# One rank product for two tiles: prefix sums made once at the head of a sort on a Trainium2 core

## The reference

```
ex1 = e * x[src];  ex2 = e * x[dst]
mi = zeros.at[dst].add(ex1);  mo = zeros.at[src].add(ex2)
h = concat([mi, mo, x]); h = tanh(h @ W1 + b1); ... four times
x = layernorm(x + h)
R = relu(edge_weight @ w1 + b1) @ w2 + b2          # per edge
msg = tensor product of R, spherical harmonics of edge_attr_3, x[src]
x = layernorm(x + zeros.at[dst].add(msg))
```

## Time and profile before

| what | value |
|---|---|
| median of 3 runs | 2183.33 us (2181.03 to 2185.21) |
| the profiled execution, its own time | 2181.47 us |
| its span, first to last instruction | 2179.7 us |
| busy in the span | PE 1313.5 (60%), DVE 1099.9 (50%), ACT 628.1 (29%), POOL 1255.6 us (58%) |
| mean granted TensorE clock | 0.741 |
| gathers L457 | 392, from 3.9 to 1205.8 us, 1.0 us each |
| scatters L462 | 392, from 65.9 to 1234.2 us, 1.0 us each |
| rank products L756, L757 | 392 each, from 63.4 to 632.2 us, granted clock 0.50 to 0.60 in 50 us stretches |

### The profile page before, as it was taken

The page is one execution under the profiler, slowest core; times in us unless marked ns, Lnnn a source line. Parts: engine busy times, 40 slices in busy tenths (PEclk is TensorE's granted clock), DMA queues, the critical chain, the costliest instruction groups (busy, mean ns, idle before and its releaser), DMA issues.

```text
span 2179.7 us, 23910 instructions
## 1 busy us (share of the span) xinstructions
PE 1313.5 (60%) x6086; PEld 938.6 (43%) x6086; DVE 1099.9 (50%) x3121; ACT 628.1 (29%) x1642; POOL 1255.6 (58%) x1315
## 2 busy tenths in 40 slices
PE   5644554232315566333332267999959999999564
PEld 4421332111113444233322155666636777777553
DVE  9543562232322222344332164777745777777576
ACT  0000000000001111000000296666634444443595
POOL 6466676666664566666666510333348888883144
PEclk8555555555557778566555598999978999999666
DMA  1011011111115555344431354455432333333486
GB/s 32 21 29 29 27 29 30 31 28 31 28 32 151 148 152 161 108 114 125 125 108 54 88 151 118 141 154 158 145 95 51 94 92 95 92 94 83 123 218 166
DMA packets 330295, 204.59 MB, mean 94 GB/s; under 512 B 32299, under 2 KB 318704, under 8 KB 330160
## 3 DMA queue, kind: packets, MB, share of 16 engines
q1 hardware_dynamic: 269008, 140.38, 24.2%
q0 software_dynamic: 35280, 49.84, 8.0%
q10 hardware_dynamic: 25872, 12.85, 2.0%
HBM read 124.03 MB, written 78.92 MB: 93 GB/s over the span
## 4 chain that ended last, share of the span: by engine, by line
issue 43%; PE 36%; DVE 8%; another core or an unknown queue 5%; POOL 4%; DVEq 2%; DMA 1%; SPq 1%; ACT 0%; POOLq 0%; ACTq 0%
PE bank L878 10%; PE bank L848 6%; PE bank L871 6%; DVE res L1083 5%; PE bank L801 3%; PE bank L803 2%; PE bank L841 2%; PE bank L839 2%; POOL out L529 2%; PE bank L887 2%; PE bank L855 2%; DVE woh L1062 2%; PE bank L811 1%; DVEq L1077 1%
## 5 line engine op out<-in xcount | busy, mean ns | idle before, releaser
L462 POOL DMA_INDIRECT placed<-pay,pos_i x392 | 395.6, 1009 | 317.2 <-issue 299.5
L457 POOL DMA_INDIRECT gat<-in_x,key_i x392 | 394.2, 1006 | 127.0 <-issue 116.4
L756 PE MATMUL bank<-oh,lower 128*128 128x196 bf16 x392 | 125.4, 338 | 301.4 <-issue 173.1
L811 PE MATMUL bank<-woh,pw 128*128 128x128 f32 x784 | 149.9, 362 | 260.5 <-DVE woh L1062 181.1
L1083 DVE TENSOR_TENSOR res<-res,bank 128x128 f32 x588 | 168.6, 287 | 258.2 <-remote 73.2
L982 DVE SCALAR_TENSOR_TENSOR junk<-iota,w_f,bank 128x196 f32<-128x196 f32 x392 | 147.7, 414 | 291.3 <-remote 158.5
L504 POOL DMA_INDIRECT gat<-x_d,src_i x196 | 256.8, 1310 | 59.5 <-issue 52.1
L811 PEld LDWEIGHTS bank<-woh,pw 128*128 128x128 f32 x784 | 136.0, 266 | 274.4 <-issue 221.6
L878 PE MATMUL bank<-prod,ident 128*128 128x280 f32 x896 | 217.8, 402 | 0.0
L756 PEld LDWEIGHTS bank<-oh,lower 128*128 128x128 bf16 x392 | 44.1, 113 | 381.1 <-issue 258.3
L878 PEld LDWEIGHTS bank<-prod,ident 128*128 128x128 f32 x896 | 171.7, 192 | 46.5 <-issue 0.6
(11 more groups left out here) (146 smaller groups left out, 2412.8 us busy)
## 6 DMA issues: line engine op xcount, KB each, us to landing
pw<-placed SPq DMA_DIRECT2D x588, 68.0 KB, 2.1
pw<-placed SPq DMA_DIRECT2D x98, 272.0 KB
xin<-in_x_t SPq DMA_DIRECT2D x98, 256.0 KB
hot_d<-woh SPq DMA_DIRECT2D x49, 256.0 KB
x_d<-res POOLq DMA_DIRECT2D x49, 256.0 KB, 3.8
oh<-hot_d SPq DMA_DIRECT2D x28, 448.0 KB
placed<-pay SPq DMA_DIRECT2D x28, 448.0 KB
out<-out ACTq DMA_DIRECT2D x49, 256.0 KB, 2.7
```

What stands on the lines that cost most here:

```text
L457: pool.indirect_dma_start(gat[:, t, :], None, x, bass.IndirectOffsetOnAxis(ap=key_i[:, 1 - c, t:t + 1], axis=0)).then_inc(s_gat[n // CHUNK ...
L462: pool.indirect_dma_start(placed[c].rearrange("t p r -> (t p) r"), bass.IndirectOffsetOnAxis(ap=pos_i[:, c, t:t + 1], axis=0), pay[i % 4][ ...
L756: pe.matmul(column(k), lower[:, :], oh[:, t, :], start=True, stop=False)
L811: ins = pe.matmul(quarter(bank, k), pw[i % 6][:, k, 0:P], woh[i % 3][:, k, :], start=True, stop=True)
```

## The change

Rank products are made for two tiles at a time: the moving operand is `oh[:, t:t + 2, :]`, 392 columns, into one PSUM bank; four such pairs are in flight, so the wait is for `place` of tile n-7. `s_rank` is counted up once for a pair. The second product is different too. A tile's sums over all tiles ahead are no longer made from `cnt_sb` and `pre` at each product. They are made once, in `sort_head`, as full sums for each row r of 49 and each of four heaps of tiles (heaps 2j and 2j+1 hold the even and odd tiles of pairs 49j to 49j+48), and copied by VectorE to `cum` as a bf16 value in partitions 0 to 63 and a bf16 remainder in partitions 64 to 112. The product then picks row r of both with a one-column matrix `pick`. `place` is as before but for the column it reads and the count that it waits for.

```
-HI, LO = 64, 96
+LO = 64
-        cnt_sb = sb_e("cnt_sb", [LO + 1, G, NW], BF16)
-        pre = sb_e("pre", [LO + 1, QT], BF16)
+        cnt_sb = sb_e("cnt_sb", [QT, 4, NW], BF16)
+        cum = sb_e("cum", [LO + QT, 2, 2 * NW], BF16)
+        pick = sb_e("pick", [LO + QT, QT], BF16)
+        under = sb_e("under", [QT, LO + QT], BF16)
+        upto = sb_e("upto", [QT, LO + QT], BF16)
...
+        def pair_of(n):
+            return psum[n // 2 % 4][:, 0:2 * NW]
+        def column(n):
+            return pair_of(n)[:, NW * (n % 2):NW * (n % 2) + NW]
+        def heap(t):
+            pair = t // 2
+            return 2 * (pair // QT) + t % 2, pair % QT
...
 count (PE)
-                    h, r = t // QT, t % QT
+                    m, r = heap(t)
...
 sort_head (PE)
-                for h in range(4):
+                for n in range(4):
                     for m in range(2):
-                        ins = pe.matmul(start_of(h), tot_sb[:, m, :], ubig[:, m, :], start=m == 0, stop=m == 1 and h == 0)
-                    for a in range(h):
-                        ins = pe.matmul(start_of(h), every[0:QT, :], cnt_sb[0:QT, a, :], start=False, stop=a == h - 1)
+                        pe.matmul(start_of(n), tot_sb[:, m, 0:LO + QT], ubig[:, m, :], start=m == 0, stop=False)
+                    for a in range(n - n % 2):
+                        pe.matmul(start_of(n), every[0:QT, 0:LO + QT], cnt_sb[:, a, :], start=False, stop=False)
+                    a = n - n % 2
+                    pe.matmul(start_of(n), (upto if n % 2 else under)[:, :], cnt_sb[:, a, :], start=False, stop=False)
+                    ins = pe.matmul(start_of(n), under[:, :], cnt_sb[:, a + 1, :], start=False, stop=True)
...
 rank (PE)
-                for k in range(G):
-                    t = G * (g % NG) + k
-                    wait(pe, s_pos, G * (g - 1) + k + 1)
-                    pe.matmul(column(k), lower[:, :], oh[:, t, :], start=True, stop=False)
-                    pe.matmul(column(k), pre[:, t % QT:t % QT + 1].broadcast_to([LO + 1, P]), cnt_sb[:, t // QT, :],
+                for k in range(0, G, 2):
+                    n, t = G * g + k, G * (g % NG) + k
+                    m, r = heap(t)
+                    wait(pe, s_pos, n - 6)
+                    pe.matmul(pair_of(n), lower[:, :], oh[:, t:t + 2, :].rearrange("p t w -> p (t w)"), start=True, stop=False)
+                    pe.matmul(pair_of(n), pick[:, r:r + 1].broadcast_to([LO + QT, P]), cum[:, m // 2, :],
                               start=False, stop=True).then_inc(s_rank, 1)
...
 constants (DVE)
-            fill.up(dve.tensor_scalar(pre[:, :], iota[0:LO + 1, 0:QT], pcol[0:LO + 1, :], None, ALU.is_gt))
+            (two comparisons for pick, two for under, two for upto)
-            fill.up(dve.memset(cnt_sb[:, :, :], 0.0))
-            done(fill)
-            for r in (HI, LO):
-                fill.up(dve.memset(pre[r:r + 1, :], 1.0))
...
 sort_starts (DVE)
-                for i in range(2):
-                    both = psum[i][:, 0:2 * NW].rearrange("p (h w) -> p h w", h=2)
-                    chain.up(dve.tensor_copy(cnt_sb[HI:LO + 1, 2 * i:2 * i + 2, :], both[HI:LO + 1]))
+                for h in range(2):
+                    chain.up(dve.tensor_copy(cum[:, h, :], psum[h][0:LO + QT, 0:2 * NW]))
                 done(chain)
-                    ins = dve.tensor_tensor(cnt_sb[LO:LO + 1, ...], both[LO:LO + 1], cnt_sb[LO:LO + 1, ...], ALU.subtract)
+                    ins = dve.tensor_tensor(cum[LO:LO + QT, h, :], psum[h][LO:LO + QT, 0:2 * NW], cum[LO:LO + QT, h, :], ALU.subtract)
...
 place (DVE)
-                    dve.wait_ge(s_rank, n + 1)
+                    dve.wait_ge(s_rank, n // 2 + 1)
-                    ... in1=column(k)
+                    ... in1=column(n)
```

More of the change, by code:

```diff
@@ L294, in quarter, with start_of @@
             return psum[bank][:, P * k:P * k + P]
[L296 to L301, removed]
+        def pair_of(n):
[5 more added lines that the diff above has]
+            return 2 * (pair // QT) + t % 2, pair % QT
+        def start_of(m):
+            return psum[m // 2][0:LO + QT, NW * (m % 2):NW * (m % 2) + NW]
         def first_rows(sp, to, c, b, landed):
@@ L544, in sort_head @@
                 act.wait_ge(s_cnt, c + 1)
-                for h in range(4):
-                    ins = act_copy(act, cnt_sb[0:QT, h, :], psum[h][0:QT, 0:NW])
+                for m in range(4):
+                    ins = act_copy(act, cnt_sb[:, m, :], psum[m][0:QT, 0:NW])
                 ins.then_inc(s_cnt_sb, 1)
@@ L717, in count @@
                 for t in range(U * n, U * n + U):
-                    h, r = t // QT, t % QT
-                    ins = pe.matmul(psum[h][0:QT, 0:NW], esel[:, QT - 1 - r:2 * QT - 1 - r], oh[:, t, :], start=r == 0, stop=r == QT - 1)
+                    m, r = heap(t)
+                    ins = pe.matmul(psum[m][0:QT, 0:NW], esel[:, QT - 1 - r:2 * QT - 1 - r], oh[:, t, :], start=r == 0, stop=r == QT - 1)
                 if n == NU - 1:
@@ L929, in _ @@
             fill.up(dve.tensor_scalar(lower[:, :], iota[:, 0:P], pcol[:, :], None, ALU.is_gt))
-            fill.up(dve.tensor_scalar(pre[:, :], iota[0:LO + 1, 0:QT], pcol[0:LO + 1, :], None, ALU.is_gt))
+            fill.up(dve.tensor_scalar(pick[0:LO, :], iota[0:LO, 0:QT], pcol[0:LO, :], None, ALU.is_equal))
+            fill.up(dve.tensor_scalar(pick[LO:LO + QT, :], iota[LO:LO + QT, 0:QT], pcol[LO:LO + QT, :], -float(LO), ALU.subtract, ALU.is_equal))
+            for a, op in ((under, ALU.is_gt), (upto, ALU.is_ge)):
+                fill.up(dve.tensor_scalar(a[:, 0:LO], iota[0:QT, 0:LO], pcol[0:QT, :], None, op))
+                fill.up(dve.tensor_scalar(a[:, LO:LO + QT], iota[0:QT, 0:QT], pcol[0:QT, :], None, op))
             fill.up(dve.memset(every[:, :], 1.0))
@@ L955, in sort_starts @@
                 dve.wait_ge(s_start, c + 1)
-                for i in range(2):
-                    both = psum[i][:, 0:2 * NW].rearrange("p (h w) -> p h w", h=2)
-                    chain.up(dve.tensor_copy(cnt_sb[HI:LO + 1, 2 * i:2 * i + 2, :], both[HI:LO + 1]))
+                for h in range(2):
+                    chain.up(dve.tensor_copy(cum[:, h, :], psum[h][0:LO + QT, 0:2 * NW]))
                 done(chain)
-                for i in range(2):
-                    both = psum[i][:, 0:2 * NW].rearrange("p (h w) -> p h w", h=2)
-                    ins = dve.tensor_tensor(cnt_sb[LO:LO + 1, 2 * i:2 * i + 2, :], both[LO:LO + 1], cnt_sb[LO:LO + 1, 2 * i:2 * i + 2, :], ALU.subtract)
+                for h in range(2):
+                    ins = dve.tensor_tensor(cum[LO:LO + QT, h, :], psum[h][LO:LO + QT, 0:2 * NW], cum[LO:LO + QT, h, :], ALU.subtract)
                 ins.then_inc(s_low, 1)
@@ L979, in place @@
                     c, t, n = g // NG, G * (g % NG) + k, G * g + k
-                    dve.wait_ge(s_rank, n + 1)
+                    dve.wait_ge(s_rank, n // 2 + 1)
                     wait(dve, s_pos, n - 3)
-                    dve.scalar_tensor_tensor(out=junk[n % 4][:, :], in0=iota[:, :], scalar=w_f[:, c, t:t + 1], in1=column(k),
+                    dve.scalar_tensor_tensor(out=junk[n % 4][:, :], in0=iota[:, :], scalar=w_f[:, c, t:t + 1], in1=column(n),
                                              op0=ALU.is_equal, op1=ALU.mult, accum_out=pos_f[:, c, t:t + 1]).then_inc(s_pos, 1)
```

## The result

| | kernel before | kernel after |
|---|---|---|
| time, median | 2183.59 us (2181.03 to 2185.21, 4 runs) | 2168.69 us (2165.59 to 2170.19, 4 runs) |
| ratio | | 0.9928, 95% interval [0.9914, 0.9941] |
| span of the profiled execution | 2179.7 us | 2163.6 us |

A forecast was written before the change was run, and what follows sets the result against it. GpSimd was taken to pace the rank stage, running dry while VectorE waits for late increments. Saving 25 us less the head's 1.6 gives -23.4 from 2181.47, so 2158.1, as a median 2160 us; range 2110 to 2187.

The forecast's parts named there:

- The bound: Rank stage: GpSimd sets the pace and runs dry at regular intervals; its holes, together 77 us, are on the path.
- What changes is the number of increments in a step: Rank stage: increments leave at the recorded times; a step needs 8, not 14, in chunk 0 and 6, not 10, in chunk 1.
- The prediction's own test: Rank stage: an unchanged number of GpSimd's holes would mean that increments were not the cost.
- if each hole grew: Rank stage: sign that the prediction is wrong; holes were to stay 4 to 5 us long.
- Chunk 0: First rank steps: a hole every third step, not every second, 5 instead of 7 over 15 steps; saves 9 us.
- Chunk 1: Later rank steps: a hole every fourth step, 6 instead of 8 over 24 steps, saves 10 us, first hole 2 more.
- The value taken: Rank stage saving: 25 us, between 21 and about 38 us, the latter if increments left every 2.0 us at any age.
- The growing intervals: Rank stage: increments leave ever later after GpSimd resumes, some 4.5 us each in the end; saving 21 us.
- The head: Before the first scatter: more bf16 sums, split fp32 sums and constants cost +1.6 us, all on the path.
- All holes close: Rival, rank stage: VectorE never falls behind, GpSimd runs at 10.26 us a step; median 2113 us, chance 0.18.
- slower: Rival, rank stage: delay goes with columns, a pair held twice as long as a tile, about 4 us; 2190 us, chance 0.10.
- Nothing comes of it: Rival, rank stage: holes needed at the same intervals whatever the increments; only the head's cost remains, 2185 us, chance 0.14.

The follow-up runs named there:

- the direct test: Kernel after with each pair's two 392-column products split into four of 196, one increment a pair, eight tiles ahead: 2021.24, 2020.96 and 2022.03 us, no delay in any.
- group 1: Four undelayed runs: kernel before with half the increments 1.0008; kernel after with extra increments 1.0020, one increment per four tiles 1.0021, four tiles ahead 1.0024.
- idle increments: Kernel after, each pair's first product also incrementing a semaphore nobody waits for: 2021.49 us without the delay, 2173.15 us with it.

## Why the prediction was right, and which of its steps was not

*The bound.* Right. GpSimd paces the stage, runs dry at regular intervals, and the time of its holes is on the path; the walks behind it moved by the same 16 us, and where the delay was absent the holes and the gain were absent with it.

*The mechanism by which the change helps.* Wrong. The failed step is "What changes is the number of increments in a step", that increments leave at the times of the rows whatever the products. With half the increments alone the time was 2186.61 us, where that step asks for 2163.5, and with the old number of them in the kernel after 2173.15, where it asks for 2183.5. The traces showed in its place that the slow part has the same pace in tiles in every variant (5 to 7 in 12 us), and that the first 8 us behind a restart hold 20 to 22 tiles, not 14, wherever the products are wide. Of the two other parts of the change, the lead accounts by the traces for 5.6 us at step 48 and not for the periods. The joined products, with the single wait of TensorE that comes with them, are what is left. That is argued and not shown: an inference by elimination from single runs on different chips, with one contrary number (2173.0), and the direct test never met the delay. Which part of the change saves the time stays open; that the number of increments alone does not is shown as far as one run each way can.

*Why it came out nearly right all the same.* By luck. The number of tiles between two holes was what mattered, and the assumed law gave nearly the right one: in chunk 0 a hole every third step, as forecast, 5 besides the first. The prediction's own test ("I am wrong if the number of holes is unchanged (then increments were not the cost)") could not tell the laws apart: joined products, lead and increments were all changed at once. Another of its signs did come true: it was to be wrong "if each hole grew", and each did, from 4.6 to 5.2 us in chunk 0 and from 5.2 to 7.0 in chunk 1. It had taken the delay to be gone 2.5 us after GpSimd's last DMA whatever came before; that is the value of chunk 0 before, and in the kernel after it was 3.6 us behind three steps and 5.5 behind five.

*Chunk 0.* Forecast -9; the holes besides the first went from 7 of 4.6 us in the mean to 5 of 5.2, which with two more ordinary gaps is -5.7; the first one, forecast to stay since it had its own cause, shrank from 4.61 to 1.20 (without the delay it was 1.79 in the kernel before and 2.05 in the kernel after); 2.2 us came back at step 24, where GpSimd now waits for chunk 1's payload (2.51 us); and 0.3 lies elsewhere. Sum -6.6.

*Chunk 1.* Forecast -12 with a hole of 4.9 us every fourth step; measured one of 7.0 every fifth, and -10.7. Of this, 3.0 us are the first hole (7.73 before, 0.77 and 4.28 after), where 2 were forecast. In idle time a step that is 1.2 forecast, 1.4 measured and 1.7 before: a hole grew with the time that it had to make good. The size is off here, the direction right.

*The value taken.* The growing intervals gave 21 and the prediction took 25; measured are 17.7 with the tail. Moving up from its own sum cost 4 of the 9 us by which the forecast missed.

*The head.* Forecast +1.6, measured +2.07: the sums 1.56 (forecast 1.3), the constants 0.23 (0.3), and 0.28 for VectorE's wait for the first pair of wide products, which the sum did not have.

*The rivals.* "All holes close" and "slower" did not happen on the chip of the result. But the premise of "slower" was right and the prediction's own wrong: in the slow part a pair is held about twice as long as a tile, at a mean interval of 4.2 us (six pairs from 187.36 to 208.50), near the 4 us that the rival named. The kernel was faster all the same, because more tiles pass before the slow part begins, which neither had. "Nothing comes of it" is what happens wherever the delay is absent: 1.0006 [0.9996, 1.0015].

The number of increments is not seen there either: in group 1 idle increments took 2021.49 us and one increment for four tiles 2021.43, with 294 fewer. The Trainium skill, page "TensorE: Matmul & The Clock Gate", section "The cost: per-tile semaphore tail", puts an increment at about 26 ns; by that these 294 would be 7.6 us, an estimate, if all of them lay on the path. The two runs differ by 0.06 us, so here they lie beside other work.

## What to carry to other kernels

A change that alters several counts at once can move the time as forecast for a reason that is not the forecast's; write down for each count what it alone would do, and undo one at a time. A stage that an engine paces with regular holes is worth its idle time a step, not its number of holes: when holes get rarer, look at whether each one grows, as here from 4.6 to 7.0 us between two steps and five. And before a gain is claimed, look at whether the loss that it cures is always there: here 0.7% is gained with it, and the head's 2 us is paid without it.

## What the runs showed of the hardware that was not expected

- The same kernel, the one before, took 2181 to 2185 us in the group of the result and in one group of experiments, 2173.0 in another (1 run), and 2016.2 to 2018.5 us (medians) in five others, one of them on a chip of the same number as the 2173.0. The difference is the delay of semaphore increments between TensorE and VectorE while GpSimd issues indirect DMAs back to back: 77 us of holes in the rank stage and 3.1 us a step in the walks, against 0.3. Step 49 started at 671.30 us with it and 595.78 without, and the rest of the kernel took 1508.4 and 1423.6.
- The delay is not a fixed latency. Behind a restart of GpSimd increments arrive at once, and from some 6 to 10 us on they come later and later: 2 us, 8 us at an age of 15 to 18, 14.5 at 33 in the kernel before, 20 at 50 in the kernel after (chunk 1). When GpSimd stops they are all there within some 2.5 us behind two steps of its DMAs, 2.9 to 3.7 behind three and 5.5 behind five.
- It is not only TensorE's increments. With eight tiles in flight, VectorE's own reached TensorE 2 to 5 us late (2.9 for the product at 191.00, 4.9 for the one at 208.61), and TensorE, VectorE and ScalarE were often released within 0.1 us of each other (at 193.80, 193.78 and 193.78).
- The DMA queues show no backlog of data over these stretches (a mean busy share of 0.10 to 0.14). What holds the increments, and what brings the delay about on some occasions and not on others, stays open.
